# Adding shared blocks ahead of gathered rows, and holding two stores, in the tail of a graph and mixture-of-experts kernel

## The chip, the cores and the metric

The kernel runs on one core of one Trainium2 chip. The metric is the device time of one execution in microseconds (us), as the median of several runs. Beside these there is one profiled execution, from which all views of the trace come; times in it count from the start of its span.

## The reference, cut to what matters

The program has two halves. The first is a relational graph convolution with a residual; the second, in which the change lies, is a mixture-of-experts layer over N = 625 tokens of D = 1024 values:

```
xf = layernorm(x)
sh = gelu(xf @ sW1[s] + sb1[s])                   # 2 shared experts
shared = mean over s of (sh @ sW2[s] + sb2[s])
gates = xf @ rW + rb                              # 8 experts
vals, idx = top_k(gates, 2);  probs = softmax(vals)
h = gelu(xf @ W1[e] + b1[e]);  y[e] = h @ W2[e] + b2[e]
moe = sum over the two chosen e of probs * y[e]
out = x + shared + moe
```

Everything is float32.

## The kernel before

Tokens lie on 128 partitions in T = 5 tiles of `rows[t]` = 128, 128, 128, 128 and 113 tokens. The accumulator `y_acc` ([128, 5, 1024] in SBUF) holds `x` when the tail begins.

The routed experts are computed on 17 tiles of 128 gathered tokens (NT = 17), each belonging to one expert. Their results go to a buffer `yrow` in HBM. When all 17 are stored, POOL issues 2T = 10 gathers from `yrow` (L673): gather k fetches for tile t = k // 2 the rows of its first or second chosen expert (j = k % 2) into a buffer of its own, `cg[k]`, six of them in the tile `big` and four in `raw`. The row numbers are in `at_i`; each of the 128 partitions gets one row of 4 KB. Semaphore `s_cg[k]` reports the landing.

Meanwhile PE computes the shared experts' second matmul, in 2T blocks of one tile and one half of the columns (`block_of(b)` is tile b // 2, half b % 2, DH = 512 columns): 12 matmuls for a block (L1517, in the helper `hilo`) and one for the biases (L1885), which ends the block and raises `f_y`. Blocks use four PSUM banks (`ps`) in turn, so block b needs that block b - 4 has been added. The last block is computed in two parts of 256 columns, and its column pieces together with the block before it are LAST_COLS: 512, 256 and 256 columns of the last tile.

DVE does all adds into `y_acc`. `add_routed(k)` (L1484) adds `cg[k]` times the gate's share `pr`, over all 1024 columns; `add_block(b)` (L1491) adds a block from PSUM, 512 columns. The last tile's blocks are added in the three pieces of LAST_COLS (L1505). The order is written out by hand: routed 0, block 0, routed 1, block 1, and so on up to block 6, then routed 7, routed 8, block 7, routed 9, and the three last pieces. One semaphore, `f_acc`, counts all adds; PE and SP wait for its counts.

SP stores finished tiles from `y_acc` to `out` (L520), each as soon as its adds are done. `row_parts(n)` splits n rows into a part that is a multiple of 16 and the rest, so the last tile's 113 rows go as 112 + 1, for each of the three column pieces. ACT has no instruction in the tail, nor has POOL but for the gathers.

Of the kernel before, what the change touches and what calls it, by code (L numbers as in the profile page):

```python
# [18 lines left out]
ALU = mybir.AluOpType  # L19
# [19 lines left out]
def program(nc, x, src, dst, rel, ln_w, w_rel, w_root, conv_b, wo, rw, rb, w1, b1, w2, b2, sw1, sb1, sw2, sb2, out):  # L39
    N, D = x.shape  # L40
    E = src.shape[0]
    R, _, F = w_rel.shape
    NE, _, HID = w1.shape
    NS = sw1.shape[0]
    NX = NE + NS
    P = 128
    T = -(-N // P)
    rows = [min(P, N - t * P) for t in range(T)]
# [20 lines left out]
    DH = D // 2  # L69
# [3 lines left out]
    def row_parts(n):  # L73

        whole = n // 16 * 16
        return [(0, whole)] + ([(whole, n - whole)] if n > whole else [])

    ctx = ExitStack()
    with ctx:
        def sb(name, shape, dt=F32):  # L80
            return ctx.enter_context(nc.sbuf_tensor(name, shape, dt))

        def sem(name):
            return ctx.enter_context(nc.semaphore(name))
# [3 lines left out]
        y_acc = sb("y_acc", [P, T, D])  # L88
# [55 lines left out]
        cg = [big[:, i * D:(i + 1) * D] for i in range(n_big)] + \  # L144
# [14 lines left out]
        yrow = nc.dram_tensor("yrow", [NT * P, D], F32).ap()  # L159
# [98 lines left out]
        at_i = sb("at_i", [P, 2, T], I32)  # L258
# [17 lines left out]
        ps = [ctx.enter_context(nc.psum_tensor(f"ps{i}", [P, 2, 512], F32)) for i in range(4)]  # L276
# [104 lines left out]
        s_cg = [sem(f"s_cg{i}") for i in range(NCG)]  # L381
# [14 lines left out]
        r_d = sem("r_d")  # L396
        r_y = sem("r_y")
        f_y = sem("f_y")
        f_acc = sem("f_acc")
        s_out = sem("s_out")  # L400

        NG, NLN = 5, 3
# [1 line left out]
        LAST_COLS = (slice(0, DH), slice(DH, DH + DH // 2), slice(DH + DH // 2, D))  # L404
# [7 lines left out]
        def _(sp):  # L412
# [83 lines left out]
            for i in range(NT):  # L496
# [15 lines left out]
                if i == SW2_AT - 1:  # L512
                    load_sw2(1)

            pieces = [(t, 4 * t + 4 + t // (T - 2), slice(0, D)) for t in range(T - 1)] \
                + [(T - 1, 4 * T - 1 + n, cols) for n, cols in enumerate(LAST_COLS)]
            for t, done, cols in pieces:
                sp.wait_ge(f_acc, done)
                for at, n in row_parts(rows[t]):
                    sp.dma_start(out[t * P + at:t * P + at + n, cols], y_acc[at:at + n, t, cols]).then_inc(s_out, 16)  # L520
            sp.wait_ge(s_out, 16 * sum(len(row_parts(rows[t])) for t, _, _ in pieces))

        N_CONST, NZ = 18, 6

# [32 lines left out]
        def _(pool):  # L557
# [6 lines left out]
            k = Tally(s_const)  # L564
# [32 lines left out]
            cols = big.shape[1] // NZ  # L597
# [71 lines left out]
            for k in range(2 * T):  # L669
                t, j = k // 2, k % 2  # L670
                if k == n_big:
                    pool.wait_ge(r_w2lo, NT)
                pool.indirect_dma_start(cg[k], None, yrow, bass.IndirectOffsetOnAxis(at_i[:, j, t:t + 1], 0)) \  # L673
                    .then_inc(s_cg[k], 16)

        def unit_views(e, second):
# [56 lines left out]
        def block_of(b):  # L733
            return b // 2, b % 2
# [3 lines left out]
        def _(act):  # L738
# [155 lines left out]
            for s in range(T + 2):  # L894
                if 2 <= s != T:
                    rows_out(s - 2)
                t = s - 1
# [10 lines left out]
                t = s - 2  # L908
# [5 lines left out]
                if s < T:  # L914
                    r = rows[s]
# [24 lines left out]
            def rows_t_out(i):  # L940

                act.wait_ge(r_t, i + 1)
                if i in ROUNDED:
                    act.activation(xg_t[:, FK * P:], ps[2][:, 1, :], ACT.Copy)
                    act.activation(xg_hl[0], ps[2][:, 0, :], ACT.Copy).then_inc(r_x, 1)
                else:
                    act.activation(xg_t, ps[2][:, :, :].rearrange("p a n -> p (a n)"), ACT.Copy).then_inc(r_x, 1)

            def w1_hi(i, ring):

                act.wait_ge(s_w1[i % NS_W], 16 * (i // NS_W + 1))
                act.wait_ge(r_u, i)
                act.activation(w1_hl[0], big[:, bass.ds(ring * UNIT, FK * HID)].rearrange("p (k n) -> p k n", k=FK),
                               ACT.Copy).then_inc(r_w1hi, 1)

            def keep_y_act(i):

                act.wait_ge(r_d, i + 1)
                if i >= 2:
                    act.wait_ge(s_yd[i % 2], 16 * (i // 2))  # L960
                else:
                    act.wait_ge(f_lo, 4)
                act.activation(y_out[i % 2][:, DH:], down_bank(i)[:, 1, :], ACT.Copy).then_inc(r_ya, 1)  # L963
                act.wait_ge(r_ya, i + 1)

            def store_y(i):
                act.wait_ge(r_y, i + 1)
                act.dma_start(yrow[i * P:(i + 1) * P, :], y_out[i % 2]).then_inc(s_yd[i % 2], 16)
# [17 lines left out]
            def ring_of(i):  # L986
                return act.value_load(tab[0:1, 2, i:i + 1], min_val=0, max_val=1)
# [25 lines left out]
            for i in range(NT):  # L1013
                ring_next = ring_of(i + 2) if i + 2 < NT else None
                if i + 2 < NT:
                    rows_t_out(i + 2)
                if i + 2 in ROUNDED:
                    w1_hi(i + 2, ring_next)
                if i != NT - 2:
                    keep_y_act(i)  # L1020
                if i + 1 < NT:
                    tile_gelu(i + 1)
                if i == NT - 2:
                    keep_y_act(i)
                if i + 2 < NT:
                    w2_hi(i + 2, ring_next)
                store_y(i)
                if i in SW2_HALVES:
                    half = SW2_HALVES.index(i)
                    raw_v, hi_v, _ = unit_views(0, True)  # L1030
                    act.wait_ge(s_sw2, 16)
                    act.activation(hi_v[:, half], raw_v[:, half], ACT.Copy).then_inc(s_hi if half else s_sw2h, 1)
                if i == SW2_AT:
                    split_hi(1, True)
                if i == 5:
                    act.wait_ge(s_b2, 96)
                    act.activation(b2_hl, b2_raw, ACT.Copy).then_inc(s_b2hi, 1)


        @block.vector  # L1040
        def _(dve):
# [102 lines left out]
            for g in range(G + LAG):  # L1144
                if g == G + 1:
                    windows, members = far_loops(dve)
                if g in LO_AT:
                    at = list(LO_AT).index(g)
# [13 lines left out]
            with dve.Fori(0, windows) as w:  # L1162
                dve.tensor_scalar(w_base[:, :], w_base[:, :], float(WD), None, ALU.add).then_inc(s_fw, 1)
                with dve.Fori(0, members) as g:
                    dve.wait_ge(s_fw, w + 1)
                    done = (w * G + g) * FAR_OPS
# [65 lines left out]
            for s in range(T + 2):  # L1232
                if 1 <= s < T:
                    elu_lo(s - 1)
                t = s - 2
# [4 lines left out]
                if s < T:  # L1240
                    r = rows[s]
# [10 lines left out]
                    for k in range(R):  # L1252
                        for at, o in agg_o[k]:
                            n = min(at + o.shape[1], F) - at
# [14 lines left out]
                t = s - 1  # L1269
# [18 lines left out]
            whole = T - 1  # L1288
# [186 lines left out]
            dve.wait_ge(s_wt, 1)  # L1475
            dve.tensor_copy(w_t[:, 0:N], ps[1][0:KB, :, :].rearrange("p a n -> p (a n)")[:, 0:N]).then_inc(s_wts, 1)

            def add_routed(k):

                t, j = k // 2, k % 2  # L1480
                r = rows[t]
                dve.wait_ge(s_cg[k], 16)
                dve.wait_ge(f_acc, 2 * k if k < 2 * T - 2 else 2 * k - 1)
                dve.scalar_tensor_tensor(y_acc[0:r, t, :], cg[k][0:r, :], pr[0:r, j, t:t + 1], y_acc[0:r, t, :],  # L1484
                                         ALU.mult, ALU.add).then_inc(f_acc, 1)

            def add_block(b):
                t, h = block_of(b)
                dve.wait_ge(f_y, b + 1)
                dve.wait_ge(f_acc, 2 * b + 1 if b < 2 * T - 3 else 2 * b + 2)  # L1490
                dve.tensor_tensor(y_acc[0:rows[t], t, h * DH:(h + 1) * DH], y_acc[0:rows[t], t, h * DH:(h + 1) * DH],  # L1491
                                  ps[2 + b % 4 // 2][0:rows[t], b % 2, :], ALU.add).then_inc(f_acc, 1)

            for b in range(2 * T - 3):
                add_routed(b)
                add_block(b)
            add_routed(2 * T - 3)
            add_routed(2 * T - 2)
            add_block(2 * T - 3)
            add_routed(2 * T - 1)  # L1500
            for n, cols in enumerate(LAST_COLS):
                dve.wait_ge(f_y, 2 * T - 1 + n)
                dve.wait_ge(f_acc, 4 * T - 2 + n)
                bank = ps[2 + n // 2][0:rows[-1], n % 2, 0:cols.stop - cols.start]
                dve.tensor_tensor(y_acc[0:rows[-1], T - 1, cols], y_acc[0:rows[-1], T - 1, cols], bank,  # L1505
                                  ALU.add).then_inc(f_acc, 1)


        @block.tensor
        def _(pe):  # L1510
# [98 lines left out]
            for g in range(G):  # L1609
                if g in (2, 13):  # L1610
                    t = 3 + g // 13
# [159 lines left out]
            for c in range(2 * T):  # L1771
                r = rows[c % T]
# [114 lines left out]
            for b in range(2 * T):  # L1887
                t, h = block_of(b)
                o = ps[2 + b % 4 // 2][0:rows[t], b % 2, :]
                if b >= 4:  # L1890
                    pe.wait_ge(f_acc, 2 * (b - 4) + 2)
                elif b == 2:
                    pe.wait_ge(r_y, NT)
                    pe.wait_ge(r_ya, NT)
                if b < 2 * T - 1:
                    shared_down(o, t, slice(h * DH, (h + 1) * DH))
                else:
                    shared_down(o[:, 0:DH // 2], t, LAST_COLS[1])
                    pe.wait_ge(f_acc, 2 * (b - 3) + 2)
                    shared_down(ps[3][0:rows[t], 0, 0:DH // 2], t, LAST_COLS[2])  # L1900
    return nc

# [20 lines left out]
```

## Time and profile before

| | us |
|---|---|
| median of 3 runs | 330.6 |
| the three runs | 329.42, 330.6, 330.65 |
| the profiled execution | 331.5 |
| its span | 328.9 |
| PE busy | 316.8 |
| DVE busy | 241.9 |
| ACT busy | 189.9 |
| POOL busy | 83.0 |

The granted clock of PE was full speed over the whole span. The page's span is the time from the first to the last instruction of the profiled execution; the execution's own time lies 2.6 us above it. The tail, from the last expert tile to the end, is the stretch from about 295 us on.

### The profile page before, as it was taken

To read this page: it belongs to the slowest core of one execution; us is meant where nothing else is said; L and a number is where in the kernel's file an instruction comes from. 1 tells how busy PE (TensorE), PEld (TensorE's weight loads), DVE (VectorE), ACT (ScalarE), POOL (GpSimd) and SP (SyncE) were. 2 spreads that over 40 slices of the span, in tenths; PEclk is the share of its full clock that TensorE was granted. 3 is DMA by queue.
4 is the path that set the end of the run, shared out by engine and by line. 5 is a ranking of instruction groups with operands and counts; after the bars stand their busy time and mean duration, and the time that the engine had idled before them with its cause. 6 is when DMAs were issued, how large, how long until landed. Compare 5 with 4: busy or idle time off the path is not lost.

```text
span 328.9 us, 6154 instructions
## 1 busy us (share of the span) xinstructions
PE 316.8 (96%) x1994; PEld 274.5 (83%) x1994; DVE 241.9 (74%) x469; ACT 189.9 (58%) x316; POOL 83.0 (25%) x94
## 2 busy tenths in 40 slices
PE   6999999999999999999999999999999999999994
PEld 2889897788789888888999888889988889878874
DVE  2999999976748456874665779977877777581975
ACT  2896999994121324442156789778877778640000
POOL 6741090001010110120213334322334320005830
PEclk9999999999999999999999999999999999999999
DMA  7970014000001125488042684989998972225993
GB/s 250 352 191 2 2 20 156 0 3 17 0 24 42 64 90 209 151 274 355 20 178 66 227 283 171 338 275 324 361 321 306 370 274 112 97 101 168 315 361 135
DMA packets 27015, 57.60 MB, mean 175 GB/s; under 512 B 2735, under 2 KB 16541, under 8 KB 26984
## 3 DMA queue, kind: packets, MB, share of 16 engines
q1 hardware_dynamic: 20458, 33.89, 30.6%
q0 software_dynamic: 3888, 14.16, 12.9%
q10 hardware_dynamic: 2638, 9.17, 7.1%
q8 instruction: 16, 0.26, 0.3%
q14 instruction: 15, 0.12, 0.1%
HBM read 66.25 MB, written 14.03 MB: 244 GB/s over the span
## 4 chain that ended last, share of the span: by engine, by line
PE 62%; ACT 10%; DMA 8%; DVE 7%; issue 5%; POOL 3%; DVEq 2%; SPq 1%; POOLq 1%; ACTq 0%
PE ps L1517 35%; PE ps L1806 10%; PE ps L1641 6%; PE ps L1795 5%; DMA y_acc<-in_x 4%; DMA raw<-yrow,at_i 3%; ACT arena_r L767 2%; POOL big L673 2%; POOL raw L673 2%; PE ps L1527 2%; DVE work L1113 2%; DVE big L1126 2%; DVEq L1129 2%; ACT sw_raw L832 1%; PE ps L1676 1%
## 5 line engine op out<-in xcount | busy, mean ns | idle before, releaser
L1517 PE MATMUL ps<-arena_r 128*128 128x512 f32 (+1 forms) x264 | 67.9, 402 | 0.5 <-DVE arena_r L1403 0.3
L1517 PE MATMUL ps<-xt,arena_r 128*128 128x314 f32 (+3 forms) x324 | 60.3, 337 | 0.0
L664 POOL DMA_INDIRECT big<-xrow,tok_i x17 | 37.0, 2175 | 88.8 <-PE ps L1795 70.0
L1517 PE MATMUL ps<-arena_r,xt 128*128 128x286 f32 (+1 forms) x360 | 59.0, 305 | 0.4 <-DVE arena_r L544 0.3
L1517 PEld LDWEIGHTS ps<-arena_r 128*128 128x128 f32 (+1 forms) x264 | 47.8, 188 | 11.6 <-DVE arena_r L1403 0.7
L1517 PEld LDWEIGHTS ps<-xt,arena_r 128*128 128x128 f32 (+1 forms) x324 | 51.2, 187 | 5.5 <-issue 0.2
L1517 PEld LDWEIGHTS ps<-arena_r,xt 128*128 128x128 f32 (+1 forms) x360 | 49.2, 187 | 1.6 <-DVE arena_r L544 0.6
L1408 DVE TENSOR_TENSOR arena_r<-raw,arena_r 128x2048 fp32r<-128x2048 f32 x17 | 38.8, 2285 | 0.8 <-ACT arena_r L994 0.7
L1806 PE MATMUL ps<-big,tile 128*128 x160 | 37.5, 380 | 0.2 <-issue 0.2
L994 ACT ACTIVATE arena_r<-raw 128x2048 fp32r x17 | 32.3, 1901 | 1.3 <-issue 0.7
L1806 PEld LDWEIGHTS ps<-big,tile 128*128 128x128 f32 x160 | 29.1, 190 | 3.7 <-issue 0.4
L1641 PE MATMUL ps<-raw,big 128*128 128x287 f32 (+7 forms) x150 | 25.9, 325 | 0.0
L1517 PE MATMUL ps<-xt 128*128 128x256 f32 x168 | 24.9, 298 | 0.0
L1641 PEld LDWEIGHTS ps<-raw,big 128*128 128x128 f32 (+2 forms) x150 | 21.7, 187 | 2.8 <-issue 0.4
L1604 PE MATMUL ps<-work,sw_raw 125*128 125x200 f16 x164 | 21.6, 252 | 2.6 <-DVE big L1126 0.6
L1113 DVE TENSOR_TENSOR work<-late,mid 125x800 f16<-125x800 f16 x40 | 22.8, 569 | 0.0
L1517 PEld LDWEIGHTS ps<-xt 128*128 128x128 f32 x168 | 22.0, 190 | 0.7
L832 ACT ACTIVATE sw_raw<-late,mid 125x128 f16<-125x128 f16 x60 | 19.6, 433 | 0.0
L1604 PEld LDWEIGHTS ps<-work,sw_raw 125*128 125x128 f16 x164 | 12.5, 98 | 7.9 <-DVE work L1113 5.7
L1436 DVE COPY tile<-ps 128x256 f32<-128x256 f32 x17 | 7.2, 426 | 16.0 <-PE ps L1517 12.7
L963 ACT ACTIVATE work<-ps 128x512 f32<-128x512 f32 x17 | 10.2, 597 | 14.9 <-PE ps L1517 14.9
L1795 PE MATMUL ps<-ident,big 128*128 128x128 f32 x136 | 17.6, 272 | 0.0
(240 smaller groups left out, 469.8 us busy)
## 6 DMA issues: line engine op xcount, KB each, us to landing
big<-in_L_ffn_W SPq DMA_DIRECT2D x19, 1024.0 KB, 7.5
raw<-in_L_ffn_W SPq DMA_DIRECT2D x19, 1024.0 KB, 11.1
yrow<-work ACTq DMA_DIRECT2D x17, 512.0 KB, 4.3
raw<-in_L_gnn_W_rel SPq DMA_DIRECT2D x2, 1144.0 KB, 10.8
y_acc<-in_x SPq DMA_DIRECT2D x4, 512.0 KB, 8.4
xrow<-work SPq DMA_DIRECT2D x4, 512.0 KB, 2.9
raw<-in_L_ffn_sW SPq DMA_DIRECT2D x2, 1024.0 KB, 5.8
sw_raw<-in_L_ffn_sW SPq DMA_DIRECT2D x2, 1024.0 KB, 10.9
```

What stands on the lines that cost most here:

```text
L664: pool.indirect_dma_start(xg[i % 2], None, xrow, bass.IndirectOffsetOnAxis(tok_i[:, i:i + 1], 0)) \
L673: pool.indirect_dma_start(cg[k], None, yrow, bass.IndirectOffsetOnAxis(at_i[:, j, t:t + 1], 0)) \
L832: ins = act.activation(src_hot[g % N_SH][:, c // 2, :, c % 2], iota_s[0:CE, :, 0], ACT.Abs, bias=neg_lo[:, g, c:c + 1])
L963: act.activation(y_out[i % 2][:, DH:], down_bank(i)[:, 1, :], ACT.Copy).then_inc(r_ya, 1)
L994: act.activation(w2_hl[i % 2][0], raw[:, bass.ds(ring * SLOT, UNIT)].rearrange("p (k n) -> p k n", k=KH), ACT.Copy).then_inc(r_w2hi, 1)
L1113: return dve.tensor_tensor(hot, columns[0:CE].rearrange("p (q k) c -> p q k c", q=1).to_broadcast(shape), index.rearrange("p (q a c) -> p ...
L1408: dve.tensor_tensor(w2_hl[i % 2][1], raw[:, bass.ds(ring * SLOT, UNIT)].rearrange("p (k n) -> p k n", k=KH), w2_hl[i % 2][0].bitcast(F32), ...
L1517: ins = pe.matmul(out_ap, a, b, start=start and k == 0, stop=stop and k == n - 1)
L1604: ins = pe.matmul(count_bank(n), src_hot[n % N_SH][:, c // 2, :, c % 2], key_hot[n % N_MH][:, c // 2, :, c % 2], start=c == 0, stop=c == C ...
L1641: ins = pe.matmul(o, a_t[0:rows[s], s, r, cols], h_rel[s][0:rows[s], r, at:at + o.shape[1]], start=start and s == tiles[0], stop=stop and ...
L1795: ins = pe.transpose(ps_rows(None)[:, k, :], xg[i % 2][:, k * P:(k + 1) * P], ident[:, :])
L1806: ins = pe.matmul(o, xg_t[:, k * P:(k + 1) * P], big[:, bass.ds(ring * UNIT + k * HID, HID)], start=k == first, stop=k == KD - 1 and first ...
```

## The change

On DVE, blocks 0, 1 and 2 are added first, then the routed rows 0, 1 and 2, then block 3, routed 3 and 4, block 4, routed 5, and so on in turn to block 7, routed 8 and routed 9, and the three last pieces. Since block adds and routed adds are no longer in one fixed interleaving, `f_acc` becomes two semaphores: `f_blk` counts block adds, `f_rtd` routed adds. PE waits for `f_blk` alone.

On SP, the store of tile 2 (and with it that of tile 3, which is behind it in the queue) also waits for the landing of gather 9. The last tile's 113th row is stored once, whole, from ACT's queue after the last add, so that SP issues three pieces instead of six. On POOL, the gathers of the last tile fetch 113 rows instead of 128.

```diff
-            pieces = [(t, 4 * t + 4 + t // (T - 2), slice(0, D)) for t in range(T - 1)] \
-                + [(T - 1, 4 * T - 1 + n, cols) for n, cols in enumerate(LAST_COLS)]
-            for t, done, cols in pieces:
-                sp.wait_ge(f_acc, done)
-                for at, n in row_parts(rows[t]):
-                    sp.dma_start(out[t * P + at:t * P + at + n, cols], y_acc[at:at + n, t, cols]).then_inc(s_out, 16)
-            sp.wait_ge(s_out, 16 * sum(len(row_parts(rows[t])) for t, _, _ in pieces))
+            for t in range(T - 1):
+                sp.wait_ge(f_rtd, 2 * t + 2)
+                sp.wait_ge(f_blk, 2 * t + 2)
+                if t == 2:
+                    sp.wait_ge(s_cg[2 * T - 1], 16)
+                sp.dma_start(out[t * P:(t + 1) * P, :], y_acc[:, t, :]).then_inc(s_out, 16)
+            whole = row_parts(rows[-1])[0][1]
+            for n, cols in enumerate(LAST_COLS):
+                sp.wait_ge(f_blk, 2 * T - 1 + n)
+                sp.dma_start(out[(T - 1) * P:(T - 1) * P + whole, cols], y_acc[0:whole, T - 1, cols]).then_inc(s_out, 16)
+            sp.wait_ge(s_out, 16 * (T - 1 + len(LAST_COLS) + len(row_parts(rows[-1])) - 1))
...
-                pool.indirect_dma_start(cg[k], None, yrow, bass.IndirectOffsetOnAxis(at_i[:, j, t:t + 1], 0)) \
+                pool.indirect_dma_start(cg[k][0:rows[t], :], None, yrow,
+                                        bass.IndirectOffsetOnAxis(at_i[0:rows[t], j, t:t + 1], 0)) \
                     .then_inc(s_cg[k], 16)
...
+            act.wait_ge(f_blk, 2 * T - 2 + len(LAST_COLS))
+            for at, n in row_parts(rows[-1])[1:]:
+                act.dma_start(out[(T - 1) * P + at:(T - 1) * P + at + n, :], y_acc[at:at + n, T - 1, :]).then_inc(s_out, 16)
...
-            for b in range(2 * T - 3):
-                add_routed(b)
-                add_block(b)
-            add_routed(2 * T - 3)
-            add_routed(2 * T - 2)
-            add_block(2 * T - 3)
-            add_routed(2 * T - 1)
+            for b in range(3):
+                add_block(b, 0)
+            for k in range(3):
+                add_routed(k, 3)
+            for b in range(3, 2 * T - 2):
+                add_block(b, b if b == 3 else b + 1)
+                if b == 3:
+                    add_routed(3, 4)
+                add_routed(b + 1, b + 1)
+            add_routed(2 * T - 1, 2 * T - 2)
...
                 if b >= 4:
-                    pe.wait_ge(f_acc, 2 * (b - 4) + 2)
+                    pe.wait_ge(f_blk, b - 3)
```

In `add_routed(k, blocks)` and `add_block(b, routed)` the second argument is the count of the other kind of add that has to be done first.

The start of DVE's tail before. Rows on `big,pr` or `raw,pr` are routed adds, rows on `ps` block adds:

```order
L1476 CAST xt<-ps 74x625 [waits s_wt]
L1484 SCALAR_TENSOR_TENSOR y_acc<-big,pr,y_acc 128x1024 [waits f_acc,s_cg0]
L1491 TENSOR_TENSOR y_acc<-y_acc,ps 128x512 [waits f_acc,f_y]
L1484 SCALAR_TENSOR_TENSOR y_acc<-big,pr,y_acc 128x1024 [waits f_acc,s_cg1]
L1491 TENSOR_TENSOR y_acc<-y_acc,ps 128x512 [waits f_acc,f_y]
L1484 SCALAR_TENSOR_TENSOR y_acc<-big,pr,y_acc 128x1024 [waits f_acc,s_cg2]
```

And the same place after:

```order
L1486 CAST xt<-ps 74x625 [waits s_wt]
L1507 TENSOR_TENSOR y_acc<-y_acc,ps 128x512 [waits f_y] x3
L1497 SCALAR_TENSOR_TENSOR y_acc<-big,pr,y_acc 128x1024 [waits f_block,s_cg0]
L1497 SCALAR_TENSOR_TENSOR y_acc<-big,pr,y_acc 128x1024 [waits f_block,f_routed,s_cg1]
L1497 SCALAR_TENSOR_TENSOR y_acc<-big,pr,y_acc 128x1024 [waits f_block,f_routed,s_cg2]
L1507 TENSOR_TENSOR y_acc<-y_acc,ps 128x512 [waits f_routed,f_y]
L1497 SCALAR_TENSOR_TENSOR y_acc<-big,pr,y_acc 128x1024 [waits f_block,f_routed,s_cg3]
```

Three block adds now stand ahead of the first routed add, and the routed adds follow each other more closely; these three blocks wait for PE alone.

SP's stores before, to the end of its program:

```order
L520 DMA out<-y_acc 128x1024 [waits f_acc] x4
L520 DMA out<-y_acc 112x512 [waits f_acc]
L520 DMA out<-y_acc 1x512
L520 DMA out<-y_acc 112x256 [waits f_acc]
L520 DMA out<-y_acc 1x256
L520 DMA out<-y_acc 112x256 [waits f_acc]
L520 DMA out<-y_acc 1x256
L79 UNCONDITIONAL_BRANCH [waits s_out]
```

And after:

```order
L521 DMA out<-y_acc 128x1024 [waits f_block,f_routed] x2
L521 DMA out<-y_acc 128x1024 [waits s_cg9,f_block,f_routed]
L521 DMA out<-y_acc 128x1024 [waits f_block,f_routed]
L525 DMA out<-y_acc 112x512 [waits f_block]
L525 DMA out<-y_acc 112x256 [waits f_block] x2
L79 UNCONDITIONAL_BRANCH [waits s_out]
```

The third store has a wait for gather 9, and the three one-row stores have left SP; one row of 1024 values stands on ACT, as its last instruction.

## Rows read from the trace of the kernel before

**Rows 1.** The page: the span, and PE's and DVE's busy time.

```profile
span 328.9 us, 6154 instructions
PE 316.8 (96%) x1994; PEld 274.5 (83%) x1994; DVE 241.9 (74%) x469; ACT 189.9 (58%) x316; POOL 83.0 (25%) x94
```

**Rows 2.** Timeline of PE: start, duration (us); the bias matmuls that end blocks.

```profile
299.80 0.40 PE L1885 MATMUL ps<-xt 74*128 74x512 f32 x1
...
317.96 0.39 PE L1885 MATMUL ps<-xt 74*128 74x512 f32 x1
...
320.97 0.40 PE L1885 MATMUL ps<-xt 74*113 74x512 f32 x1
...
322.62 0.28 PE L1885 MATMUL ps<-xt 74*113 74x256 f32 x1
...
324.16 0.28 PE L1885 MATMUL ps<-xt 74*113 74x256 f32 x1
```

**Rows 3.** Timeline of DVE in the tail; in brackets the idle time before.

```profile
294.25 0.80 DVE L1476 CAST xt<-ps 74x625 fp32r<-74x625 f32 x1
302.85 1.29 DVE L1484 SCALAR_TENSOR_TENSOR y_acc<-big,pr,y_acc 128x1024 f32<-128x1024 f32 x1 [7.80 <-DMA big<-yrow,at_i]
304.24 0.69 DVE L1491 TENSOR_TENSOR y_acc<-y_acc,ps 128x512 f32<-128x512 f32 x1
305.05 1.28 DVE L1484 SCALAR_TENSOR_TENSOR y_acc<-big,pr,y_acc 128x1024 f32<-128x1024 f32 x1
...
318.52 1.28 DVE L1484 SCALAR_TENSOR_TENSOR y_acc<-raw,pr,y_acc 128x1024 f32<-128x1024 f32 x1 [0.48 <-DMA raw<-yrow,at_i]
320.66 1.28 DVE L1484 SCALAR_TENSOR_TENSOR y_acc<-raw,pr,y_acc 113x1024 f32<-113x1024 f32 x1 [0.86 <-DMA raw<-yrow,at_i]
...
322.98 1.28 DVE L1484 SCALAR_TENSOR_TENSOR y_acc<-raw,pr,y_acc 113x1024 f32<-113x1024 f32 x1 [0.24 <-DMA raw<-yrow,at_i]
324.36 1.74 DVE L1505 TENSOR_TENSOR y_acc<-y_acc,ps 113x512 f32<-113x512 f32 x3
```

**Rows 4.** The chain that ended last, its final part: start, duration, what.

```profile
314.00 8.96 DMA raw<-yrow,at_i
...
325.68 0.42 DVE y_acc L1505
```

**Rows 5.** Timeline of POOL: gathers 0, 3, 4, 5 and 9.

```profile
298.44 0.94 POOL L673 DMA_INDIRECT big<-yrow,at_i  x1 [29.13 <-DMA yrow<-work]
...
302.18 0.94 POOL L673 DMA_INDIRECT big<-yrow,at_i  x1 [0.30 <-issue]
303.42 1.53 POOL L673 DMA_INDIRECT big<-yrow,at_i  x1 [0.30 <-issue]
305.25 1.89 POOL L673 DMA_INDIRECT big<-yrow,at_i  x1 [0.30 <-issue]
...
314.00 1.87 POOL L673 DMA_INDIRECT raw<-yrow,at_i  x1 [0.30 <-issue]
```

**Rows 6.** Timeline of POOL and of DVE around an earlier gather.

```profile
231.78 3.02 POOL L664 DMA_INDIRECT big<-xrow,tok_i  x1 [4.71 <-PE ps L1795]
...
231.69 2.29 DVE L1408 TENSOR_TENSOR arena_r<-raw,arena_r 128x2048 fp32r<-128x2048 f32 x1 [0.47 <-ACT arena_r L994]
...
234.50 1.22 DVE L1428 TENSOR_TENSOR xt<-big,xt 128x1024 fp32r<-128x1024 f32 x1
```

**Rows 7.** Timeline of SP's queue: the last tile's first, fifth and last issues.

```profile
325.08 0.34 SPq L520 DMA_DIRECT2D out<-y_acc  x1
...
326.55 0.66 SPq L520 DMA_DIRECT2D out<-y_acc  x2
...
326.91 0.30 SPq L520 DMA_DIRECT2D out<-y_acc  x1
```

**Rows 8.** Windows: length, engines' busy time, clock, then DMA share and GB/s.

```profile
300.00:321.00 21.00, 21.00 (x92) 16.78 (x91) 15.44 (x16) 0.00 (x0) 13.43 (x9) 1.00 0.91 322
...
319.00:320.00 1.00, 1.00 (x6) 0.76 (x5) 0.80 (x1) 0.00 (x0) 0.00 (x0) 1.00 1.06 434
```

More of the change, by code:

```diff
@@ L398, in program @@
         f_y = sem("f_y")
-        f_acc = sem("f_acc")
+        f_blk = sem("f_block")
+        f_rtd = sem("f_routed")
         s_out = sem("s_out")
@@ L1476, in _, with add_routed @@
             dve.tensor_copy(w_t[:, 0:N], ps[1][0:KB, :, :].rearrange("p a n -> p (a n)")[:, 0:N]).then_inc(s_wts, 1)
-            def add_routed(k):
+            def add_routed(k, blocks):
                 t, j = k // 2, k % 2
@@ L1482, in add_routed @@
                 dve.wait_ge(s_cg[k], 16)
-                dve.wait_ge(f_acc, 2 * k if k < 2 * T - 2 else 2 * k - 1)
+                if k:
+                    dve.wait_ge(f_rtd, k)
+                if blocks:
+                    dve.wait_ge(f_blk, blocks)
                 dve.scalar_tensor_tensor(y_acc[0:r, t, :], cg[k][0:r, :], pr[0:r, j, t:t + 1], y_acc[0:r, t, :],
-                                         ALU.mult, ALU.add).then_inc(f_acc, 1)
-            def add_block(b):
+                                         ALU.mult, ALU.add).then_inc(f_rtd, 1)
@@ L1488, in add_block @@
+            def add_block(b, routed):
                 t, h = block_of(b)
+                r = rows[t]
                 dve.wait_ge(f_y, b + 1)
-                dve.wait_ge(f_acc, 2 * b + 1 if b < 2 * T - 3 else 2 * b + 2)
-                dve.tensor_tensor(y_acc[0:rows[t], t, h * DH:(h + 1) * DH], y_acc[0:rows[t], t, h * DH:(h + 1) * DH],
-                                  ps[2 + b % 4 // 2][0:rows[t], b % 2, :], ALU.add).then_inc(f_acc, 1)
-            for b in range(2 * T - 3):
-                add_routed(b)
-                add_block(b)
@@ L1497, in _ @@
-            add_routed(2 * T - 3)
-            add_routed(2 * T - 2)
-            add_block(2 * T - 3)
-            add_routed(2 * T - 1)
+                if routed:
+                    dve.wait_ge(f_rtd, routed)
+                dve.tensor_tensor(y_acc[0:r, t, h * DH:(h + 1) * DH], y_acc[0:r, t, h * DH:(h + 1) * DH],
+                                  ps[2 + b % 4 // 2][0:r, b % 2, :], ALU.add).then_inc(f_blk, 1)
+            for b in range(3):
+                add_block(b, 0)
+            for k in range(3):
+                add_routed(k, 3)
@@ L1501, in _ @@
+            for b in range(3, 2 * T - 2):
[4 more added lines that the diff above has]
+            add_routed(2 * T - 1, 2 * T - 2)
             for n, cols in enumerate(LAST_COLS):
                 dve.wait_ge(f_y, 2 * T - 1 + n)
-                dve.wait_ge(f_acc, 4 * T - 2 + n)
+                dve.wait_ge(f_rtd, 2 * T)
                 bank = ps[2 + n // 2][0:rows[-1], n % 2, 0:cols.stop - cols.start]
@@ L1505, in _ @@
                 dve.tensor_tensor(y_acc[0:rows[-1], T - 1, cols], y_acc[0:rows[-1], T - 1, cols], bank,
-                                  ALU.add).then_inc(f_acc, 1)
+                                  ALU.add).then_inc(f_blk, 1)
         @block.tensor
@@ L1898, in _ @@
                     shared_down(o[:, 0:DH // 2], t, LAST_COLS[1])
-                    pe.wait_ge(f_acc, 2 * (b - 3) + 2)
+                    pe.wait_ge(f_blk, b - 2)
                     shared_down(ps[3][0:rows[t], 0, 0:DH // 2], t, LAST_COLS[2])
```

## Prediction

> **What bounds the kernel now.** I read the page first. PE is busy for 96% of the span, DVE for far less [rows 1], so the span as a whole is PE's. But the change touches only the last 30 us, and a share of busy time says nothing about which wait ends last there. So I went to the timeline of each engine in that stretch.
>
> PE first [rows 2]. The ten shared blocks run without a break: one ends every 3.03 us (block 1 at 300.20, block 7 at 318.35, block 8 at 321.37), then the two half-width parts of block 9 at 322.90 and 324.44. PE waits for nobody there, so 324.44 is a floor that nothing in this change can move.
>
> DVE next [rows 3]. It stands idle for 7.80 us from 295.05, until the first gathered row tile has landed at 302.8, although blocks 0 and 1 have been ready since 297.2 and 300.2. Then it alternates a routed add (1.28 us, with its gap 1.39) and a block add (0.69, with its gap 0.81), 2.20 us for a pair, and waits for a gather three more times: 0.48, 0.86 and 0.24 us. The tenth routed add starts at 322.98, because gather 9 was issued at 314.00 and landed 8.96 us later; the chain of waits runs through exactly that transfer, and ends with the last quarter add at 325.68 + 0.42 = 326.10 [rows 4]. That is 1.66 us after PE's floor. Ahead of it stand the three last adds: the third could have started at 324.47 and starts at 325.68.
>
> SP last [rows 7]. The last tile goes out as three column pieces, each of 112 rows and 1 row: six issues from 325.08, one every 0.36 us. They form a queue, so the third piece leaves at 326.55 (0.45 us after its data are ready) and the last row at 326.91. From there to the end of the span are 2.35 and 1.99 us.
>
> **Part 1: three blocks first.** DVE adds blocks 0 and 1 while it would be idle; they cost nothing. Block 2 is ready at 300.20 + 3.03 = 303.23 and added by 303.95. So routed add 0, which began at 302.85, now begins at 304.0: a delay of 1.15 us for the routed rows, against three block adds (3 x 0.81 = 2.4 us) taken out of what follows. From 304.0: eight routed adds (0 to 7) and blocks 3 to 6 are 8 x 1.39 + 4 x 0.81 = 14.4 us, so 318.4, just when block 7 is ready (318.35). Block 7 to 319.2, routed adds 8 and 9 to 322.0, the half add of block 8 to 322.8, the first quarter waits for PE (322.90) and ends at 323.4, the second waits for PE (324.44) and ends at 324.47 + 0.42 = 324.9. If the gathers keep up, DVE ends 1.2 us earlier and PE bounds it. The slack: the last quarter starts on time if routed add 9 ends by 324.47 - 0.53 - 0.80 = 323.15, so DVE has 1.1 us, and gather 9 may land as late as 321.85. The third semaphore wait on a routed add is one more short sequencer step, some hundredths of a microsecond in each of ten: hidden in the slack. PE waits for block adds alone; block 4 needs the add of block 0, and the nearest case (block 9) needs block 6 at 322.9, which is added about 317: no stall.
>
> **Part 2: when do the gathers land.** Two things move them. First, DMA: between 300 and 321 the engines are 0.91 busy at 322 GB/s [rows 8], so the gathers stand in a queue, and the store of tile 2 (0.52 MB) stood in it too. Holding it back takes 0.52 MB / 322 = 1.6 us off (1.2 at the 434 GB/s of the best microsecond); tile 3 was issued after the gathers anyway. That alone gives a landing between 321.3 and 321.7, inside the slack by 0.1 to 0.5 us. The 15 rows fewer in gathers 8 and 9 are 0.12 MB, another 0.3 us: 321.1 by the mean rate, if the engines are kept as busy as before. Second, POOL [rows 5]: a gather takes it 0.94 us while DVE is idle, but 1.53 and then 1.88 from the moment routed adds run. A gather that starts inside a routed add ends 0.8 us after that add does. The earlier gather of 3.02 us that starts with a long DVE add (231.69 to 233.98) and ends at 234.80 shows the same 0.82 [rows 6]. So before, one gather goes through per pair, 2.2 us each. Now the routed adds stand closer: if one gather passes per routed add, gather 9 leaves POOL at about 312.5 instead of 315.9. If back-to-back adds leave no opening (bound from the other side), it passes one per cluster and leaves at 319.0; gather 0 landed 3.4 us after POOL was done with it, so 322.4, and routed add 9 ends at 323.7, 0.55 us past the slack. I take the first, since with each add 0.1 us of gap comes by.
>
> The Trainium skill (SBUF — State Buffer, "Who interferes with whom") says that a DVE instruction with two SBUF inputs contends with a GpSimd instruction that reads SBUF, and that whichever starts first blocks the other fully. The rows agree with its first half, POOL held by DVE. By its second half DVE could be held as well, the slower rival below.
>
> **Part 3: the stores.** Tiles 2 and 3 leave SP once gather 9 has landed and block 7 is added, so at 319.2 to 321.7, followed by the first column piece at 322.8. Together these and the rest of tile 4 are 1.5 MB, 3.5 to 4.6 us: done between 322.8 and 326.3. SP now issues three pieces instead of six with nothing in between, so the last one leaves at 324.92. The single row (4 KB whole) goes out on ACT, which has nothing after 295, at about the same time. Queued behind SP's new wait are only stores. The tail after the last issue is 1.99 to 2.35 us by the two rows of before. **Sum:** last add 326.10 to 324.90 is -1.2; issue behind it -0.4 (or -0.8 if the single row was what ended last): -1.6 to -2.0, and I take -1.7, nearer to the larger piece. Span 328.9 to 327.2. The profiled execution took 331.5, 0.9 over the median of the runs, so I take the difference to the median: 330.6 - 1.7 = 328.9.
>
> **Rivals.** (a) *The held stores become the end.* If gather 9 lands only at 321.7 and the 1.5 MB move at 322 GB/s, the last column piece queues behind them and its bytes move at about 326.4: gain 1.1, time 329.5. The starved POOL of part 2 gives the same. For it: the mean rate. Against: the DMA engines go idle after 321 in the trace and reached 434 GB/s with stores in it.
>
> (b) *The 113-row gather runs on few engines: slower.* Every gather of before has 128 rows, so no row shows what 113 cost. 434 GB/s over 16 engines is 27 GB/s for one, and 113 rows of 4 KB on one engine are 0.46 MB / 27 = 17 us, against about 1.2 us now. That is 15.9 us over the eight rows that an engine moves of such a gather now: both would land at 321.1 + 15.9 = 337.0; then one routed add and the last three adds (3.0) and the store (2.3): span 342.3, time 344.0; more if both fall on the same engine. It decides from about 24 rows on one engine: 16 over the eight are 2.4 us, which use up the 0.75 us from 321.1 to 321.85 and the 1.7 gained. In the code the plain loads and stores split off the 113th row, which says that there the row count mattered; the gather isn't split. For: nothing in the trace of a gather. Against: all 27 gathers have a row per partition, and a gather is written row by row from a list, for which an even division isn't needed. The Trainium skill (DMA: Bandwidth & Descriptors, "Why a DMA increments its semaphore by 16 and not by 1") speaks for it: a DMA uses the largest number of engines up to 16 that divides its rows, which for 113 is 1; it excepts some direct copies from GpSimd and says nothing of indirect ones. No run here shows it.
>
> (c) *POOL holds DVE.* If each of gathers 4 to 9 stops a routed add for its 0.94 us, that is 5.6 us, 4.5 over the slack of 1.1: span 327.2 + 4.5 = 331.7, time 333.4. Against it: gather 3 was in progress (302.18 to 303.12) when routed add 0 started, and that add took its normal 1.29 [rows 3, 5]; so did the 1.22 us add at 234.50 [rows 6].
>
> **How the numbers follow.** Forecast 0.69, rival (a) 0.16, (b) 0.12, (c) 0.03. The likeliest is 328.9. Its own range is -1.4 to -2.3, 328.3 to 329.2; with (a), and the spread of the three runs (329.4 to 330.7), 328.2 to 330.3, which leaves out (b) and (c). Half a per cent, about what a measurement of this kernel can tell from no change, is 1.65 us, 328.95: the forecast lies on this line. So somewhat over half of its 0.69 and a little of (a) count as faster, 0.46; the rest of both as the same, 0.39; (b) and (c) as slower, 0.15.
>
> **What would show it.** In the changed trace: two DVE adds before 301, routed add 0 at 304.0, no wait of DVE for a gather of note, the last add ending at 324.9, set by PE; POOL's last gather ending near 312.5; the last SP store issued within 0.1 us of the last add; span 327.2. I am wrong if the last two gathers take over 10 us to land (b), if routed adds are longer than 1.4 us beside POOL (c), or if the last piece needs more than 2.4 us from issue to end (a).

## The result and the profile after

| | before | changed |
|---|---|---|
| median (us) | 330.01 | 343.9 |
| runs (us) | 329.05 to 330.65 | 343.17 to 344.37 |
| span of the profiled execution (us) | 328.9 | 341.7 |

The ratio to the kernel before is 1.042, with a 95% interval of 1.0385 to 1.0459: slower by 14 us. (The kernel before has a fourth run here, 329.05; that is why its median is below the 330.6 of three runs.) The forecast was 328.9. The case that came true is rival (b), for which the prediction had worked out 344.0 and given a chance of 0.12.

The timeline of DVE in the changed kernel (start, duration, and in brackets the idle time before) answers to [rows 3]:

```profile
303.02 0.69 DVE L1507 TENSOR_TENSOR y_acc<-y_acc,ps 128x512 f32<-128x512 f32 x1 [2.33 <-PE ps L1904]
303.82 1.29 DVE L1497 SCALAR_TENSOR_TENSOR y_acc<-big,pr,y_acc 128x1024 f32<-128x1024 f32 x1
305.33 2.68 DVE L1497 SCALAR_TENSOR_TENSOR y_acc<-big,pr,y_acc 128x1024 f32<-128x1024 f32 x2 [0.22 <-DMA big<-yrow,at_i]
...
318.69 0.69 DVE L1507 TENSOR_TENSOR y_acc<-y_acc,ps 128x512 f32<-128x512 f32 x1
333.64 1.28 DVE L1497 SCALAR_TENSOR_TENSOR y_acc<-raw,pr,y_acc 113x1024 f32<-113x1024 f32 x1 [14.26 <-DMA raw<-yrow,at_i]
335.64 1.28 DVE L1497 SCALAR_TENSOR_TENSOR y_acc<-raw,pr,y_acc 113x1024 f32<-113x1024 f32 x1 [0.72 <-DMA raw<-yrow,at_i]
337.03 1.35 DVE L1524 TENSOR_TENSOR y_acc<-y_acc,ps 113x512 f32<-113x512 f32 x3
```

Up to block 7 at 318.69 everything runs close to the forecast (routed add 0 at 303.82, forecast 304.0; block 7 at 318.69, forecast 318.4). Then DVE waits 14.26 us for gather 8 and 0.72 us for gather 9, which are exactly the two gathers that fetch 113 rows. The chain of waits says the same in one row (start, duration, what), where [rows 4] had 8.96:

```profile
312.78 22.84 DMA raw<-yrow,at_i
```

Why is that transfer slow? In the windows (length, busy time of PE, PEld, DVE, ACT, POOL, clock, DMA share, GB/s) the DMA engines are nearly idle while DVE waits, unlike in [rows 8]:

```profile
314.00:315.00 1.00, 1.00 (x6) 0.82 (x5) 0.69 (x1) 0.00 (x0) 1.00 (x1) 1.00 1.05 366
...
321.00:322.00 1.00, 1.00 (x10) 1.00 (x9) 0.00 (x0) 0.00 (x0) 0.00 (x0) 1.00 0.13 53
322.00:323.00 1.00, 1.00 (x11) 1.00 (x10) 0.00 (x0) 0.00 (x0) 0.00 (x0) 1.00 0.13 53
...
332.00:333.00 1.00, 0.00 (x0) 0.00 (x0) 0.00 (x0) 0.00 (x0) 0.00 (x0) 0.50 0.12 49
```

A share of 0.13 is two engines of 16 (2 / 16 = 0.125), and 53 GB/s over two engines is 26 GB/s for each, nearly the 27 GB/s (434 / 16) that one engine has when all are busy [rows 8]. Two gathers are in flight: one engine each. The page's row for POOL's DMA queue shows a second trace of it, its number of packets (queue, kind, packets, MB, share); before it was 3888:

```profile
q0 software_dynamic: 7248, 14.05, 12.5%
```

3888 packets for 27 gathers are 144 for each of 128 rows, that is 16 x (8 + 1). Take 25 of these away from 7248, and the two gathers of 113 rows have 1824 each: 16 x (113 + 1). So the count is what it would be if each of the 16 engines were given as many packets as the one that carries the most, here all 113 rows, and one more. The trace doesn't show which packet is on which engine, but the added ones carry next to nothing: the page counts 3388 more packets under 512 bytes (6123 against 2735) and 30 fewer of 4 KB. POOL takes 3.3 us for such a gather here (start, duration; compare [rows 5]):

```profile
304.93 1.00 POOL L678 DMA_INDIRECT big<-yrow,at_i  x1 [0.31 <-issue]
306.23 1.20 POOL L678 DMA_INDIRECT raw<-yrow,at_i  x1 [0.30 <-issue]
307.74 1.09 POOL L678 DMA_INDIRECT raw<-yrow,at_i  x1 [0.30 <-issue]
309.13 3.34 POOL L678 DMA_INDIRECT raw<-yrow,at_i  x1 [0.30 <-issue]
312.78 3.26 POOL L678 DMA_INDIRECT raw<-yrow,at_i  x1 [0.30 <-issue]
```

PE runs out of work at 324.2. Its granted clock is still 1.00 in the windows up to 328 and 0.50 (1.2 of 2.4 GHz) from 329 on, as in the last window above; nothing waits for PE by then.

### The profile page after: what moved, and what is told of

Read it like the earlier page. It is cut to its first block, busy times and chain, and to the rows that moved or that the text cites. A ratio compares the mean times of both kernels' runs of the same rounds, so it can differ in the third digit from the quotient of the medians.

```text
span 341.7 us, 6153 instructions
## 1 busy us (share of the span) xinstructions
PE 317.9 (93%) x1994; PEld 274.8 (80%) x1994; DVE 241.8 (71%) x469; ACT 189.8 (56%) x316; POOL 82.6 (24%) x94
## 2 busy tenths in 40 slices
DMA packets 30371, 57.49 MB, mean 168 GB/s; under 512 B 6123, under 2 KB 19927, under 8 KB 30340
## 3 DMA queue, kind: packets, MB, share of 16 engines
q0 software_dynamic: 7248, 14.05, 12.5%
## 4 chain that ended last, share of the span: by engine, by line
PE 59%; DMA 11%; ACT 9%; DVE 7%; issue 5%; POOL 3%; DVEq 3%; SPq 1%; POOLq 0%; ACTq 0%
PE ps L1536 34%; PE ps L1825 9%; DMA raw<-yrow,at_i 7%; PE ps L1660 5%; PE ps L1814 4%; DMA y_acc<-in_x 4%; ACT arena_r L773 2%; POOL raw L678 2%; DVEq L1139 2%; PE ps L1546 2%; DVE big L1136 2%; ACT sw_raw L838 1%; POOL big L678 1%; DVE work L1123 1%; PE ps L1695 1%
```

## The experiments

Theory E: the two gathers of 113 rows run on one engine each, and all the loss is theirs; the rest of the change does what the prediction said. Rivals: H, the held stores or the closer order of the adds delay the gathers; F, any gather of fewer than 128 rows is slow.

### Undo the 113 rows alone (undo_rows)

```diff
-                pool.indirect_dma_start(cg[k][0:rows[t], :], None, yrow,
-                                        bass.IndirectOffsetOnAxis(at_i[0:rows[t], j, t:t + 1], 0)) \
+                pool.indirect_dma_start(cg[k], None, yrow, bass.IndirectOffsetOnAxis(at_i[:, j, t:t + 1], 0)) \
```

> The changed kernel, but the last tile's two gathers fetch 128 rows again instead of 113; everything else of the change stays. Theory E (a gather of 113 rows is carried by one DMA engine, and nothing else in the change costs time): the last gather lands at about 321 us, no wait of DVE for it of note, the last add ends at 324.9, set by PE, span 327.2, time 1.7 us under the kernel before (ratio 0.995). Rival H (the held stores, or the closer order of gathers and adds, are what delays): the last gather still lands well after 325 and the time stays above that of the kernel before.

Measured: 328.76 us, ratio 0.9954 (0.9938 to 0.9971), span 327.1. One line of the change makes up all of the loss; what is left is a gain of 1.4 to 1.5 us. The end of DVE's timeline:

```profile
318.97 0.69 DVE L1506 TENSOR_TENSOR y_acc<-y_acc,ps 128x512 f32<-128x512 f32 x1
319.79 2.66 DVE L1496 SCALAR_TENSOR_TENSOR y_acc<-raw,pr,y_acc 113x1024 f32<-113x1024 f32 x2
322.56 1.02 DVE L1523 TENSOR_TENSOR y_acc<-y_acc,ps 113x512 f32<-113x512 f32 x2
324.35 0.42 DVE L1523 TENSOR_TENSOR y_acc<-y_acc,ps 113x256 f32<-113x256 f32 x1 [0.77 <-PE ps L1903]
```

Routed adds 8 and 9 follow without a wait for a gather, and the last quarter add now waits for PE and ends at 324.77 (forecast 324.9). H falls.

### The 113 rows alone in the kernel before (only_rows)

```diff
-                pool.indirect_dma_start(cg[k], None, yrow, bass.IndirectOffsetOnAxis(at_i[:, j, t:t + 1], 0)) \
+                pool.indirect_dma_start(cg[k][0:rows[t], :], None, yrow,
+                                        bass.IndirectOffsetOnAxis(at_i[0:rows[t], j, t:t + 1], 0)) \
```

> The kernel before, and only the last tile's two gathers cut from 128 to 113 rows. Theory E: gather 9 is issued at about 314 as before and lands 22 to 24 us later, at 336 to 338; then one routed add, the three last adds and the six issues of SP (about 6 us): span 342 to 344, ratio 1.04. The DMA share is about 0.13 (two engines of 16) while DVE waits. Rival H: span near 329, ratio 1.00, since no store is held and the order is the old one.

Measured: 347.02 us, ratio 1.0497 (1.0463 to 1.0531), span 345.2. The mechanism is confirmed without any of the rest, and it is more expensive than expected (span 342 to 344, ratio 1.04), and than in the changed kernel. Gather 8 landed later than there (337.08 against 333.64): POOL issued it 1.9 us later (311.06 against 309.13), since with the old order one gather goes through every 2.2 us, and it needed 26.0 us from there instead of 24.5. This kernel doesn't hold the stores of tiles 2 and 3; the next experiment prices that. The DMA share in the wait is the same two engines:

```profile
337.08 1.28 DVE L1485 SCALAR_TENSOR_TENSOR y_acc<-raw,pr,y_acc 113x1024 f32<-113x1024 f32 x1 [18.36 <-DMA raw<-yrow,at_i]
```

```profile
326.00:336.00 10.00, 0.00 (x0) 0.00 (x0) 0.00 (x0) 0.00 (x0) 0.00 (x0) 0.60 0.13 52
```

### No held store, with 113 rows (rows113_no_hold)

```diff
-                if t == 2:
-                    sp.wait_ge(s_cg[2 * T - 1], 16)
```

> The changed kernel as it is, with 113 rows, but the store of tile 2 doesn't wait for the last gather. The gathers land as before, gather 9 at 335 to 336, since at 0.12 of the DMA engines' time there was room for stores. Tiles 2 and 3 are then stored while DVE waits, and the end follows the last add by 2.3 us as with 128 rows, and not by the 3.4 us of the changed kernel: span 340.7, about 1 us less than the changed kernel, ratio to the kernel before 1.039. If the held stores were without effect, the ratio is 1.042 as with the change.

Measured: 346.33 us, ratio 1.0512 (1.0482 to 1.0541), span 343.6. A miss, and in the other direction. Against the kernel before, run beside each, the changed kernel lost 13.9 us and this one 16.5. Gathers 8 and 9 let their adds start at 335.84 and 338.03, not at 333.64 and 335.64:

```profile
335.84 1.29 DVE L1495 SCALAR_TENSOR_TENSOR y_acc<-raw,pr,y_acc 113x1024 f32<-113x1024 f32 x1 [16.78 <-DMA raw<-yrow,at_i]
338.03 1.29 DVE L1495 SCALAR_TENSOR_TENSOR y_acc<-raw,pr,y_acc 113x1024 f32<-113x1024 f32 x1 [0.90 <-DMA raw<-yrow,at_i]
```

The end did follow the last add more closely, as expected: that add ended at 340.77, 2.8 us before the end of the span, against 338.38 and 3.3 us with the hold. But I had argued from the mean share, 0.12, that there was room for the stores. There is room on fourteen engines; on the two that carry the gathers there is none. The store of tile 3, issued at 319.14, keeps all 16 engines busy:

```profile
320.00:321.00 1.00, 1.00 (x7) 0.77 (x6) 0.00 (x0) 0.00 (x0) 0.00 (x0) 1.00 1.00 410
```

Spread evenly, its 128 rows are eight on each engine, and 8 x 0.16 = 1.3 us (an estimate); the two stores together are 2.6 us. From issue to landing gather 8 took 27.0 us instead of 24.5, and gather 9 25.6 instead of 22.8, so 2.5 and 2.7 us more, which fits. So the held stores, nearly worthless with 128 rows, saved about 2.5 us of the damage of the 113.

### No held store, with 128 rows (undo_rows_hold)

The same two lines are taken out of undo_rows.

> As undo_rows, and the store of tile 2 no longer waits for the last gather. If the held store matters as the prediction has it, the last gather lands about 1.2 to 1.6 us later than in undo_rows, at about 321.4 to 322.7, which costs 0 to 0.9 us at the end: ratio to the kernel before 0.995 to 0.998. If the gathers are no longer near the limit at all, the time is that of undo_rows within 0.3 us, or less, since tiles 2 and 3 are out of the way of the last pieces.

Measured: 329.04 us, ratio 0.9964 (0.9943 to 0.9986), span 326.9. The last add ends at 324.60. The second case holds: no difference to undo_rows that can be told. Routed adds 8 and 9 follow without a wait in both kernels, so the gathers are no longer near the limit, held store or not.

### Other numbers of rows (rows120, rows118, rows116, rows114)

```diff
-                pool.indirect_dma_start(cg[k][0:rows[t], :], None, yrow,
-                                        bass.IndirectOffsetOnAxis(at_i[0:rows[t], j, t:t + 1], 0)) \
+                pool.indirect_dma_start(cg[k][0:(P if t < T - 1 else 120), :], None, yrow,
+                                        bass.IndirectOffsetOnAxis(at_i[0:(P if t < T - 1 else 120), j, t:t + 1], 0)) \
```

The others have 118, 116 and 114 in place of 120. The further rows land in partitions that nothing reads.

> The changed kernel with 120 rows instead of 113 in the last tile's two gathers (the seven further rows land in partitions that nothing reads). Theory E with the even division (the number of engines is the largest up to 16 that divides the rows: 15 for 120, 8 rows each): as fast as undo_rows within 0.5 us, ratio 0.995, last gather at about 321. Rival F (any gather of fewer than 128 rows takes a slow way, row by row on one engine): last gather after 335 and ratio about 1.045. Rival G (rows are dealt out in eights from the first engine on, whatever their number): also fast, but then 113 could not have been slow.

> The changed kernel with 118 rows (2 x 59) in the last tile's two gathers. If the number of engines is the largest up to 16 that divides the rows, each gather runs on 2 engines with 59 rows each. The 113-row gathers moved a row in about 0.16 us on their engine, so gather 9 lands 54 x 0.16 = 8.6 us earlier than their 335.6: at about 327, after which one routed add, the last adds and the stores need 6 us: span 332 to 334, ratio 1.010 to 1.020, DMA share near 0.25 (4 engines of 16) in the wait. If instead every number of rows that isn't a multiple of eight falls to one engine, the ratio is 1.045, as with 113.

> The changed kernel with 116 rows (4 x 29) in the last tile's two gathers. By the even division each runs on 4 engines with 29 rows: 21 rows over the eight of a 128-row gather are 3.4 us, so gather 9 lands at 322 to 323.5, just past the slack of DVE: last add 0.2 to 1.5 us after PE's floor, ratio 0.996 to 1.000. By one engine for what is no multiple of eight: 1.045.

> The changed kernel with 114 rows (6 x 19) in the last tile's two gathers. The even division gives 6 engines with 19 rows each. The profiles so far show 16 x (rows on an engine + 1) packets for such a gather (1824 with 113, 960 with 118, 480 with 116, 144 with 120 and 128), so here 320 each, and 3600 + 640 = 4240 packets on POOL's DMA queue. At 0.16 us a row as with 113 and 118, gather 9 lands at about 321.3; at the 0.27 us seen with 116, about 2.7 us before the 322.8 of that run. Either is inside DVE's slack: ratio 0.995 to 0.998. Against the division (one engine): 1.04.

The row of 128 is undo_rows, that of 113 the changed kernel. The engines are what the division gives; the packets are counted.

| rows | engines by even division | rows on one | packets on q0 | (packets - 3600) / 2 | ratio (interval) |
|---|---|---|---|---|---|
| 128 | 16 | 8 | 3888 | 144 = 16 x 9 | 0.9954 (0.9938 to 0.9971) |
| 120 | 15 | 8 | 3888 | 144 = 16 x 9 | 0.9975 (0.9952 to 0.9998) |
| 118 | 2 | 59 | 5520 | 960 = 16 x 60 | 1.0139 (1.0107 to 1.0171) |
| 116 | 4 | 29 | 4560 | 480 = 16 x 30 | 1.0089 (1.0055 to 1.0124) |
| 114 | 6 | 19 | 4240 | 320 = 16 x 20 | 1.0009 (0.9988 to 1.003) |
| 113 | 1 | 113 | 7248 | 1824 = 16 x 114 | 1.042 (1.0385 to 1.0459) |

The packet rows of 118, 116 and 114, each from its own kernel:

```profile
q0 software_dynamic: 5520, 14.08, 12.4%
```

```profile
q0 software_dynamic: 4560, 14.06, 13.1%
```

```profile
q0 software_dynamic: 4240, 14.04, 13.0%
```

The packet counts fit the even division in all six cases, though nearly the same number of bytes moves; with 120 rows they can't tell 15 engines from 16, as the busiest has eight rows either way. 120 rows are fast, so F falls. G (rows dealt out in eights) falls too, since 118, 116 and 114 rows would then need no more packets than 120; so does one engine for every number that is no multiple of eight. The windows of 118 show four engines at nearly their full rate, 98 GB/s:

```profile
318.00:319.00 1.00, 1.00 (x6) 0.78 (x5) 0.90 (x2) 0.00 (x0) 0.00 (x0) 1.00 0.26 98
```

118 came out as expected (334.63 us, span 333.4; gather 9 let its add start at 327.35). 116 and 114 missed, both on the slow side. With 116 the share, 0.55, is that of eight engines or nearly nine, and they move 135 GB/s, 17 for each of eight engines instead of 26:

```profile
318.00:319.00 1.00, 1.00 (x6) 0.77 (x5) 0.58 (x1) 0.00 (x0) 0.00 (x0) 1.00 0.55 135
```

That is 0.24 us a row instead of 0.16. Gather 9 had landed by 323.06, when the held store of tile 2 was issued, as expected (322 to 323.5). But gather 8 had only just landed as well, and let its add start at 322.84. Two routed adds were left and not one, so the last add ended at 326.95, 1.0 us past the latest that I expected. The held stores, released at the same time, were then in the queue ahead of the last pieces, and the end followed 2.8 us later instead of 2.3. These two make 1.5 us of the 2.6 by which 332.66 us lies over the kernel before, where I had put at most nothing; the rest isn't settled.

With 114 the adds started at 320.66. By the slack of the prediction (gather 9 by 321.85, so gather 8 one add earlier, by 320.46) that is 0.2 us too late, yet the last add still ended at 324.85, at PE's floor (PE ends at 324.38 here): the three last adds need less than Part 1 gave them. The span is 327.6 all the same and no gain is left (330.19 us):

```profile
320.66 2.66 DVE L1497 SCALAR_TENSOR_TENSOR y_acc<-raw,pr,y_acc 113x1024 f32<-113x1024 f32 x2 [1.25 <-DMA raw<-yrow,at_i]
323.42 1.43 DVE L1524 TENSOR_TENSOR y_acc<-y_acc,ps 113x512 f32<-113x512 f32 x3
```

From its last add to the end are 2.8 us against 2.3 in undo_rows, which would be rival (a) in small: the stores of tiles 2 and 3 were issued from 320.89 instead of 319.35. That explains 0.5 us. Each taken against the kernel before that was run beside it, 114 rows are 1.8 us worse than undo_rows (+0.4 and -1.4), and the rest of that isn't settled.

### The order alone, and the stores alone (order_only, store_only)

order_only is the kernel before with the new order of adds (the DVE and PE parts of the change, and SP waiting for the two semaphores); store_only has only this, in the kernel before, and the ACT part with `act.wait_ge(f_acc, 4 * T - 2 + len(LAST_COLS))`:

```diff
             for t, done, cols in pieces:
                 sp.wait_ge(f_acc, done)
-                for at, n in row_parts(rows[t]):
-                    sp.dma_start(out[t * P + at:t * P + at + n, cols], y_acc[at:at + n, t, cols]).then_inc(s_out, 16)
+                whole = row_parts(rows[t])[0][1]
+                sp.dma_start(out[t * P:t * P + whole, cols], y_acc[0:whole, t, cols]).then_inc(s_out, 16)
```

> The kernel before with nothing changed but the order of DVE's adds (and the two semaphores that go with it): 128-row gathers, no held store, the last row in three pieces on SP as before. The last add ends at PE's floor, 1.2 us earlier. SP has issued the first two column pieces and their rows by then, so the third piece leaves at once: nearly the whole 1.4 us of undo_rows, ratio 0.995 to 0.9965. If the stores were what gave the gain instead, the ratio is 0.998 to 1.

> The kernel before with nothing changed but the last tile's stores: three pieces of 112 rows on SP, the single row whole on ACT after the last add; DVE's order, the 128-row gathers and the stores of tiles 0 to 3 as before. The last add ends where it did (326.1), the last piece is issued 0.4 us earlier than before: gain 0.3 to 0.5 us, ratio 0.9985 to 0.999. If the six issues on SP were the real limit of the end, the gain is 1 us or more.

Measured: order_only 329.07 us, ratio 0.9976 (0.9955 to 0.9996), span 326.9; store_only 329.58 us, ratio 0.9983 (0.9968 to 0.9999), span 327.9. The last adds of the two kernels:

```profile
324.18 0.42 DVE L1520 TENSOR_TENSOR y_acc<-y_acc,ps 113x256 f32<-113x256 f32 x1 [1.02 <-PE ps L1900]
```

```profile
323.71 1.74 DVE L1509 TENSOR_TENSOR y_acc<-y_acc,ps 113x512 f32<-113x512 f32 x3
```

With the order alone DVE waits for PE and ends at 324.60; with the stores alone it doesn't, and ends at 325.45. The medians give 1.0 and 0.45 us (from 330.03), together 1.4, the gain of undo_rows; the intervals are wide beside this (0.1 to 1.5 us for the order, 0 to 1.1 for the stores), so that the parts add up is no more than consistent. Both ratios lie just outside what was expected (0.995 to 0.9965, and 0.9985 to 0.999), and both intervals reach into it.

No kernel beats undo_rows beyond its interval. It is the version to keep, with or without the held stores; its gain is 0.3 to 0.6% by the interval.

## Why the prediction was right or wrong

**The step that failed** is in Part 2 and in the chances. Part 2 books the 113 rows as a saving of 0.3 us (0.12 MB fewer), puts the landing of gather 9 at 321.1, and the forecast's sum has no wait of DVE for it. Each such gather in fact took 22.8 to 24.5 us from issue to landing, where the prediction had named over 10 us as the sign of (b): one DMA engine carried all its rows. DVE waited 15 us, and the term that was booked as -0.3 cost 15 us of the kernel's time (343.9 against 328.76). The price was worked out in rival (b): landing at 337.0, measured 335.64; span 342.3, measured 341.7; time 344.0, measured 343.9. So the cost of the case was known, and what was wrong was to leave it out of the sum with a chance of 0.12. I let two weak arguments outweigh a rule: that all 27 gathers seen had a row per partition (all of them had 128 rows, so they could say nothing of 113), and that a list of rows needs no even division (an idea of how gathers work, with no row behind it). For (b) stood the code, which splits 113 into 112 + 1 in its plain loads and stores of token tiles, and the Trainium skill (DMA: Bandwidth & Descriptors, "Why a DMA increments its semaphore by 16 and not by 1"), by whose rule 113 rows get one engine. The runs agree with that rule for gathers from POOL: by the DMA share with 113 and 118 rows (0.13 and 0.26 with two gathers in flight), and by the packets at one, two, four and six engines.

**Part 1, the order:** right. Routed add 0 started at 303.82 in the changed kernel (304.0). In undo_rows the last add ended at 324.77 (324.9), bound by PE, and routed add 9 ended at 322.45 (322.0), 0.7 us before the slack ran out.

**Part 2, POOL:** right in the reading that a gather that starts inside a routed add ends 0.82 us after it, and that one passes between two back-to-back routed adds. In undo_rows gather 8 starts inside the first of the two routed adds that run from 308.90 (the first ends at 310.18) and ends at 311.00, and the last gather leaves POOL at 311.30 + 1.07 = 312.37 (312.5):

```profile
309.09 1.91 POOL L678 DMA_INDIRECT raw<-yrow,at_i  x1 [0.30 <-issue]
311.30 1.07 POOL L678 DMA_INDIRECT raw<-yrow,at_i  x1 [0.30 <-issue]
```

The gathers landed earlier than the 321.1 from the mean rate. Gather 9 in undo_rows had landed by 319.35, when the store that waits for it was issued (start, duration on SP's queue):

```profile
319.35 0.81 SPq L521 DMA_DIRECT2D out<-y_acc  x2
```

Part 2 took the 322 GB/s that the kernel before moved on average; undo_rows moves 414 to 426 GB/s from 311 to 317. The held store was given 1.2 to 1.6 us at the landing, which no run shows by itself; with 128 rows it is worth nothing at the end, as the slack covers it, and about 2.5 us with 113.

**Part 3, the sum:** near without the 113 rows: -1.7 forecast, -1.4 by the medians. The profiled spans differ by 1.8 (328.9 to 327.1), but that of the kernel before lies high: the median span of its 28 runs beside undo_rows is 327.8, and that of undo_rows 326.7, so -1.1. The last add came 1.2 us earlier by forecast and 1.3 by the two traces (326.10 to 324.77). That the last piece left SP 0.45 us after its data was worth 0.45 us by store_only (0.4).

**Rival (a)** is not the case that came true, but the changed kernel shows it: from last add to end 3.3 us instead of 2.3, with the stores of tiles 2 and 3 issued from 335.69, behind the last gather. From the issue of the last piece (338.65) to the end are 3.0 us, over the 2.4 that the prediction named as its sign; in undo_rows they are 2.3 (from 324.80). The gain of 1.1 us that the prediction gave this rival doesn't follow from the 326.4 beside it: the time from there to the end isn't stated. **Rival (c)** fell: no routed add was longer than 1.29 us beside POOL, so DVE held POOL and never POOL DVE.

## What to carry to other kernels

Before you trim a transfer to the rows that are needed, divide: what counts is the rows on the busiest DMA engine, and two gathers of 113 rows made the kernel 15 us longer than two of 128, though they move fewer bytes. Where nothing in a trace has the shape that a change introduces, rows of another shape are no evidence for it, and a chance of 0.12 for a known rule against an untried shape is far too little. A mean DMA share hides where the work is: at 0.13 two engines were full, and two more stores cost about 2.5 us.

## What was not expected of the hardware

- A gather that doesn't divide evenly has 16 x (rows on the busiest engine + 1) packets, 1824 instead of 144. POOL's time grows with them: the last gather takes it 1.07, 1.10, 1.26, 1.63 and 3.26 us with 128, 114, 116, 118 and 113 rows (144, 320, 480, 960 and 1824 packets), though a part of it can be the wait for a routed add; in only_rows it was 2.35 us for 113 rows.
- The short packets seem to cost the engines time as well: from 315 to 316 they are 0.93 busy in the changed kernel at 91 GB/s, and from 317 to 318 0.57 busy at 37 GB/s. No run separates this.
- Gathers on 8 engines in sum (116 rows) moved a row in 0.24 us on each, those on two or four in 0.16. With 114 rows (12 engines in sum) it is slow too: 184 GB/s at a share of 0.73, from 318 to 319, is 16 GB/s for each busy engine, 0.26 us a row. Why is open.
- In every kernel with the new order, one block add waits 0.46 us where PE had been done for 2 us and the routed add ahead of it is named as the releaser. It isn't on the path, and its cause stays open:

```profile
314.27 0.69 DVE L1507 TENSOR_TENSOR y_acc<-y_acc,ps 128x512 f32<-128x512 f32 x1 [0.46 <-DVE y_acc L1497]
```
